# Routing the second FFN's first group of tokens inside the attention rounds

## What is computed

```python
logits = xf @ Wg
top_w, top_i = jax.lax.top_k(logits, TOP_K)
top_w = jax.nn.softmax(top_w, axis=-1)
...
h = jnp.einsum('nc,ech->enh', xf, W1)
g = jnp.einsum('nc,ech->enh', xf, W2)
y = jnp.einsum('enh,ehc->enc', jax.nn.silu(h) * g, W3)
out = jnp.einsum('enc,ne->nc', y, combine)
```

## Time and profile before

| | us |
|---|---|
| median of 3 runs | 816.96 |
| the runs | 812.55 to 818.23 |
| the profiled execution's own time | 811.2 |
| its span, first to last instruction | 809.4 |
| busy PE, DVE, ACT, POOL | 530.4, 531.9, 413.3, 204.9 |
| attention's DVE work ends at | 648.5 |
| the second FFN's block starts at | 670.4 |

### The profile page before, as it was taken

The page is one execution under the profiler, slowest core; times in us unless marked ns, Lnnn a source line. Parts: engine busy times, 40 slices in busy tenths (PEclk is TensorE's granted clock), DMA queues, the critical chain, the costliest instruction groups (busy, mean ns, idle before and its releaser), DMA issues. The chain is left out here.

```text
span 809.4 us, 14477 instructions
## 1 busy us (share of the span) xinstructions
PE 530.4 (66%) x5186; PEld 439.2 (54%) x5186; DVE 531.9 (66%) x1210; ACT 413.3 (51%) x909; POOL 204.9 (25%) x195
## 2 busy tenths in 40 slices
PE   5367567575666379999832578888868803878730
PEld 4256566464566278899832444454544503878720
DVE  2989989999996225575624477888875304654734
ACT  5576766778852254477633436767654202333320
POOL 1111221222215312607045240000000070163444
PEclk9567868867777769999975668999985655999985
DMA  8354456554562301223111400000000011134322
GB/s 242 79 150 122 145 156 172 156 151 124 155 170 83 99 7 57 72 70 106 43 43 26 157 0 1 2 2 1 2 1 1 1 49 43 49 97 114 86 69 58
DMA packets 98891, 63.96 MB, mean 79 GB/s; under 512 B 57218, under 2 KB 89476, under 8 KB 98692
## 3 DMA queue, kind: packets, MB, share of 16 engines
q1 hardware_dynamic: 94564, 54.12, 23.3%
q0 software_dynamic: 4256, 8.92, 3.8%
HBM read 40.33 MB, written 22.68 MB: 78 GB/s over the span
## 5 line engine op out<-in xcount | busy, mean ns | idle before, releaser
L1866 DVE TENSOR_REDUCE mx<-s_ps 128x2 f32<-128x512 f32 x128 | 82.4, 687 | 28.3 <-PE s_ps L1627 28.2
L1803 ACT ACTIVATE pt<-st_ps 128x512 f32<-128x512 f32 x128 | 69.7, 600 | 36.2 <-PE st_ps L1637 35.4
L336 POOL DMA_INDIRECT xd<-xs_all,r_posA x32 | 33.4, 1044 | 201.2 <-DVE r_posA L320 192.1
L1269 ACT ACTIVATE hid<-up,wblk 128x128 f32<-128x128 f32 x184 | 52.9, 375 | 49.6 <-PE up L1168 49.6
L630 ACT ACTIVATE tap<-cst_s,par 128x328 f32<-128x328 f32 x128 | 72.3, 654 | 3.8 <-DVE par L994 3.8
L637 ACT ACTIVATE rest<-rest,par 128x264 f32<-128x264 f32 x128 | 53.7, 504 | 29.9 <-DVE rest L941 29.9
L618 POOL TENSOR_TENSOR kst<-kst 128x504 f32<-128x504 f32 x16 | 16.4, 1026 | 181.3 <-DVE kst L869 181.3
L1627 PE MATMUL s_ps<-kf,qf 32*128 32x256 f32 x256 | 34.7, 349 | 31.0 <-DVE mx L1866 25.8
L336 POOL DMA_INDIRECT xd<-xs_all,r_posB x32 | 33.9, 1059 | 76.0 <-DVE r_posB L320 66.9
L1168 PE MATMUL up<-xsT,wblk 128*128 128x128 f32 x368 | 52.2, 288 | 0.0
L2145 DVE COPY wblk<-wslab 128x768 f32 x46 | 26.8, 585 | 38.1 <-issue 23.6
(11 more groups left out here) (364 smaller groups left out, 1375.5 us busy)
## 6 DMA issues: line engine op xcount, KB each, us to landing
kd<-kst SPq DMA_DIRECT2D x16, 512.0 KB, 3.0
xc<-in_x_coarse SPq DMA_DIRECT2D x16, 512.0 KB, 4.2
yd<-eos SPq DMA_DIRECT2D x44, 128.0 KB, 1.9
xsb<-xd SPq DMA_DIRECT2D x20, 256.0 KB, 3.4
wslab<-in_w SPq DMA_DIRECT2D x8, 578.0 KB, 4.7
dW<-kd SPq DMA_DIRECT2D x16, 256.0 KB, 3.3
wslab<-in_w SPq DMA_DIRECT2D x1, 3072.0 KB, 10.4
xd<-zero_t SPq DMA_DIRECT2D x2, 1472.0 KB, 11.1
```

The lines of the kernel that those rows point to most:

```text
L336: nc.gpsimd.indirect_dma_start(out=rows, out_offset=bass.IndirectOffsetOnAxis(ap=R.pos[:, t, k:k + 1], axis=0), in_=x[:, R.first + t, :], ...
L1269: nc.scalar.activation(hid[j % 2][:, k, :], up_ps[j % 2][:, k * P:(k + 1) * P], ACT.Gelu, bias=wblk[j % 4][:, 2 * DF + k:2 * DF + k + 1]). ...
L1803: nc.scalar.activation(pt[h % 8][:].rearrange("p t q -> p (t q)"), st_ps[k][:], ACT.Exp, scale=SCALE)\
L1866: nc.vector.tensor_reduce(mx[:, :, h:h + 1], s_ps[k][:].rearrange("p (t k) -> p t k", t=2), AX, ALU.max).then_inc(s_used, 1)
```

## The change

Group A of the second FFN is routed two rounds earlier. Its eight tiles are final when `projected(3)` has run at the head of round 6. In round 6 come the variances, the root (ACT, behind the fifth pair of exponentials), the rows, and the turning and columns of the first half; in round 7 the second half, the logits, largest, chosen, counted, prefix, ends and slots; in round 8 the owners. As `s_ps` is still in use then, all of it goes through the one bank `x_ps[2]`, half by half: a new function, `half_rows_turned`, turns four tiles into it. PE's `maxima`, which use that bank too, now wait in round 7 for the first columns and in round 8 for the positions. In the second FFN, B's turning moves from ahead of A's first rows to behind `up(1)`; DVE takes B's variances ahead of the first three `expert` copies and the columns behind `gated(0)`; logits and largest come at block 1, counted at 2, prefix and ends at 3, slots at 4, owners at 5.

```diff
--- before.py
+++ after.py
@@ -235,6 +235,14 @@
 
     v.wait_ge(R.turned, k + 1)
     nc.vector.tensor_copy(R.cols[:, k * CH:(k + 1) * CH], banks[k][:]).then_inc(R.cols_set, 1)
+
+
+def half_rows_turned(nc, pe, R, x, bank, k, ident):
+
+    pe.wait_ge(R.rows_set, 1)
+    for t in range(4 * k, 4 * k + 4):
+        last = nc.tensor.transpose(bank[:, t % 4 * P:(t % 4 + 1) * P], x[:, R.first + t, :], ident[:])
+    last.then_inc(R.turned, 1)
 
 
 def route_logits(nc, pe, R, bank, gate):
@@ -1697,6 +1705,10 @@
                     else:
                         pe.wait_ge(row_used, 1)
                     project(4 * i + 6)
+                if i == B - 1:
+                    pe.wait_ge(routes[0].cols_set, 1)
+                if i == B:
+                    pe.wait_ge(routes[0].pos_set, 1)
                 if i - 1 in whole:
                     pe.wait_ge(proj_used, min(4 * i + 6, PROJ))
                     maxima(i - 1, 1, 2)
@@ -1711,6 +1723,9 @@
                     project(4 * i + 7)
                 scores(i, 2)
                 values(i - 1, 0)
+                if i == B - 1:
+                    pe.wait_ge(max_added, 2 * i)
+                    half_rows_turned(nc, pe, routes[0], xs_all, x_ps[2], 1, ident)
                 scores(i, 3)
                 if i - 2 in whole:
                     if 4 * i + 6 < PROJ:
@@ -1723,10 +1738,9 @@
                     else:
                         pe.wait_ge(pj_used, i - 2)
                     by_token(i - 2, 1, 1)
-                if i == B:
-                    second_turned(nc, pe, routes[0], xs_all, s_ps, ident)
-                if i == B + 1:
-                    route_prefix(nc, pe, routes[0], s_ps[1], tri)
+                if i == B - 1:
+                    pe.wait_ge(ffn1_in, 32)
+                    route_logits(nc, pe, routes[0], x_ps[2], wgs)
                 scores(i, 4)
                 if 4 * i + 8 < PROJ:
                     if i >= 1:
@@ -1749,9 +1763,10 @@
                         pe.wait_ge(proj_used, 4 * i + 8)
                     value_rows(i + 1, 1)
                 scores(i, 6)
-                if i == B:
-                    pe.wait_ge(ffn1_in, 32)
-                    route_logits(nc, pe, routes[0], s_ps[0], wgs)
+                if i == B - 2:
+                    half_rows_turned(nc, pe, routes[0], xs_all, x_ps[2], 0, ident)
+                if i == B - 1:
+                    route_prefix(nc, pe, routes[0], x_ps[2], tri)
                 if 4 * i + 9 < PROJ:
                     pe.wait_ge(proj_used, 4 * i + 9)
                     project(4 * i + 9)
@@ -1823,13 +1838,13 @@
                 powers(i - 1, 0)
                 high(4 * i + 6)
                 powers(i - 1, 1)
-                if i == B:
-                    second_root(nc, act, routes[0], 1)
                 outputs(i - 2, 1)
                 high(4 * i + 7)
                 powers(i - 1, 2)
                 powers(i - 1, 3)
                 powers(i - 1, 4)
+                if i == B - 2:
+                    second_root(nc, act, routes[0], 1)
                 high(4 * i + 8)
                 powers(i - 1, 5)
                 if i + 1 in whole:
@@ -1916,40 +1931,44 @@
                     split(3)
                 projected(i - 3)
                 if i == B:
-                    second_variances(nc, link, routes[0], xs_all)
-                if i == B + 1:
-                    route_largest(nc, v, link, routes[0], s_ps[0], None)
-                    route_chosen(nc, link, routes[0])
-                    route_counted(nc, v, link, routes[0], it8)
+                    route_owners(nc, link, routes[0], blk, WROW)
                 largest(i, 1)
                 if i == 0:
                     split(4)
                     split(5)
                 split(4 * i + 6)
                 add_maxima(i - 1, 1, 2)
-                if i == B:
-                    second_rows(nc, v, link, routes[0], xs_all)
-                    for k in range(2):
-                        second_columns(nc, v, routes[0], s_ps, k)
                 largest(i, 2)
                 split(4 * i + 7)
+                if i == B - 2:
+                    second_variances(nc, link, routes[0], xs_all)
                 largest(i, 3)
+                if i == B - 1:
+                    second_columns(nc, v, routes[0], (None, x_ps[2]), 1)
                 if i == 0:
                     v.wait_ge(va_set, 6)
                 negated(i, 0)
                 largest(i, 4)
                 averaged(i - 2)
-                if i == B + 1:
-                    route_ends(nc, v, link, routes[0], s_ps[1])
-                    route_slots(nc, link, routes[0], s_ps[1])
-                    route_owners(nc, link, routes[0], blk, WROW)
+                if i == B - 1:
+                    route_largest(nc, v, link, routes[0], x_ps[2], None)
                 largest(i, 5)
+                if i == B - 2:
+                    second_rows(nc, v, link, routes[0], xs_all)
+                if i == B - 1:
+                    route_chosen(nc, link, routes[0])
+                    route_counted(nc, v, link, routes[0], it8)
                 split(4 * i + 8)
                 largest(i, 6)
                 add_maxima(i, 0, 0)
                 largest(i, 7)
                 split(4 * i + 9)
                 negated(i, 1)
+                if i == B - 2:
+                    second_columns(nc, v, routes[0], (x_ps[2],), 0)
+                if i == B - 1:
+                    route_ends(nc, v, link, routes[0], x_ps[2])
+                    route_slots(nc, link, routes[0], x_ps[2])
             projected(B - 1)
             v.wait_ge(row_added, 1)
 
@@ -2063,18 +2082,19 @@
                                             start=(k == 0), stop=(k == 1))
                 last.then_inc(eo_ready, 1)
 
-            second_turned(nc, pe, second, xs_all, rt_ps, ident)
             rows_turned(0)
             for j in range(TOTAL + 1):
                 if j < TOTAL:
                     if plan.opens(j) and pair_of[j] + 1 < len(PAIRS):
                         rows_turned(pair_of[j] + 1)
                     up(j)
+                if j == 1:
+                    second_turned(nc, pe, second, xs_all, rt_ps, ident)
                 if j >= 1:
                     down(j - 1)
-                if j == 0:
+                if j == 1:
                     route_logits(nc, pe, second, rt_ps[0], wgs)
-                if j == 4:
+                if j == 3:
                     route_prefix(nc, pe, second, rt_ps[1], tri)
 
         @block.scalar
@@ -2159,32 +2179,32 @@
                                                    R.rs[:, 0, t:t + 1], ALU.subtract, ALU.mult)
                 last.then_inc(y_ready, 1)
 
+            second_variances(nc, link, second, xs_all)
             for j in range(3):
                 expert(j)
-            second_variances(nc, link, second, xs_all)
+            second_rows(nc, v, link, second, xs_all)
             route_shares(nc, v, first)
-            second_rows(nc, v, link, second, xs_all)
-            for k in range(HALVES):
-                second_columns(nc, v, second, rt_ps, k)
             for j in range(TOTAL + 2):
                 if j < TOTAL:
                     gated(j)
+                if j == 0:
+                    for k in range(HALVES):
+                        second_columns(nc, v, second, rt_ps, k)
                 if j + 3 < TOTAL:
                     expert(j + 3)
-                if j == 0:
+                if j == 1:
                     route_largest(nc, v, link, second, rt_ps[0], None)
-                if j == 1:
                     route_chosen(nc, link, second)
                 if j == 2:
                     route_counted(nc, v, link, second, it8)
+                if j == 3:
+                    route_ends(nc, v, link, second, rt_ps[1])
                 if j == 4:
+                    route_slots(nc, link, second, rt_ps[1])
+                if j == 5:
+                    route_owners(nc, link, second, blk, WROW)
+                if j == 6:
                     route_shares(nc, v, second)
-                if j == 5:
-                    route_ends(nc, v, link, second, rt_ps[1])
-                if j == 6:
-                    route_slots(nc, link, second, rt_ps[1])
-                if j == 7:
-                    route_owners(nc, link, second, blk, WROW)
                 for m in range(first.n // 2):
                     if j == NB + 7 + 3 * m:
                         link(route_pair(nc, v, link, first, xs_all, m))
```

## The result

The changed kernel has a median of 777.20 us over four runs (775.47 to 779.75), the kernel before 815.92 beside it; the ratio is 0.953, 95% interval 0.948 to 0.958. Two later comparisons of the same two kernels gave 0.959 (0.954 to 0.963) and 0.957 (0.950 to 0.963), so it is 33 to 39 us faster; 29.1 were forecast, at 787.9 us.

What follows compares the result with a forecast made beforehand. Waits on POOL's scatters were taken to bound the kernel: some 22 us after attention, 5.28 in the second FFN. Block start -19.4 and B's rows -9.7 sum to -29.1, giving 787.9 us, range 776 to 800.

Steps and rivals of the forecast that it cites:

- round 6: Attention: added variances +2.4, root and rows together +1.3, columns and transposes nothing; +3.7 us, bounds 2.5 and 7.7.
- round 7: Attention: columns and logits +2.4, largest +1.1, chosen and counted +0.6, prefix +1.7, ends and slots nothing; +5.8 us.
- rounds 8 and 9: Attention without A's routing: transposes -1.8, logits -2.1, root and table loads -1.8, round 9 -1.9; -7.6 us, bounds -12 and -4.
- end of attention to the next block: With the scatter hidden, the next block starts about 0.5 us behind attention's own end, where some 22 us were waited.
- that to B's rows: Second FFN, block start to B's rows in PE: 50.0 us instead of 59.7, so -9.7; bounds -4 and -12.
- B's rows to the end: Second FFN, from B's rows in PE to the end of the span: 79.4 us, taken as unchanged.
- The hidden scatter: POOL's scatter of A runs beside rounds 8 and 9, ends near 642.6; next block starts at about 651.0 instead of 670.36.
- The second FFN: B's first scatter 24.2 us into the block instead of 33.8, B's rows at 50.0; the 5.28 us stall mostly goes.
- The rule on GpSimd's transfers: Scatters beside VectorE copies: by the skill's factor 4.8 us each, both scatters some 60 us longer; trace intervals grew 7%.
- the slow rival: Scatters beside VectorE slow, at 2.41 + 0.30 us each: span end 820.5, median 828 us. Chance 0.02.
- Half clock through round 7: Rival: PE at half clock all through round 7 costs 7 to 8 us more: 795.5 us. Chance 0.22.
- The added routing fits into idle time: Rival: rounds 6 and 7 cost 5 us instead of 9.5, block starts at 646.5: 783 us. Chance 0.2.

Runs made afterwards that it cites:

- repeats: The changed kernel unaltered, measured twice more beside other kernels on one chip: 781.89 us, ratio 0.959, and 779.83 us, ratio 0.957.
- without the variances: Changed kernel with group A's variances taken earlier, six tiles' statistics in round 5, the rest behind projected(3): 772.92 us, ratio 0.952.
- three pieces of round 8: Three kernels, each the changed kernel with one piece put back in round 8, result unread: root 779.84 us, logits 779.93, transposes 780.35.
- the scatter uncovered: Changed kernel, but POOL waits for the last projection's sum before scattering A, routing staying in rounds 6 and 7: 799.54 us, ratio 0.983.
- both edits: Changed kernel with the variances taken early and round 7's logits issued behind the fifth scores: 776.61 us, ratio 0.955.

## Why the prediction was right

The terms, in us, as forecast and as three profiles of the changed kernel show them:

| step | forecast | first profile | repeats |
|---|---|---|---|
| round 6 | +3.7 | +3.5 | +3.5, +3.5 |
| round 7 | +5.8 | +4.9 | +6.9, +6.9 |
| rounds 8 and 9 | -7.6 | -10.4 | -8.8, -8.8 |
| end of attention to the next block | -21.3 | -21.6 | -21.6, -21.6 |
| that to B's rows | -9.7 | -10.3 | -10.2, -10.0 |
| B's rows to the end | 0 | -1.0 | -1.1, -0.9 |
| sum | -29.1 | -35.0 | -31.3, -30.9 |

- *What bounds the kernel* was right, and so was the mechanism: both waits on a scatter are gone, and each pays alone.
- *The hidden scatter*: POOL was to start at 621.7 + 0.85 and end with 5.6 us to spare. It ended 2.9 us ahead of where it would have decided (644.76 + 2.24 against 649.92), 4.6 in the repeats, as rounds 8 and 9, which cover it, were shorter than forecast.
- *Round 6*: the total held, its split didn't. The root and the rows were put at 1.3; without the variances round 6 has its old length, the seventh maxima coming 1.5 later at full clock (591.62 - 577.95 = 13.7 against 587.39 - 575.25 = 12.1) and the rest being repaid, as the clock doesn't fall where it fell before. The variances were put at 2.4 and cost 3.5 with the clock that went with them. That the sum came out at 3.5 against 3.7 is in part luck: one term too small and one too large.
- *Round 7*: within the terms at either clock. The columns and logits ahead of the fifth scores cost the hole of 2.51 that 2.4 were set for; taking them away gave 1.5. The prefix, put at +0.9 at full clock and +2.7 at half, left DVE waiting 0.90 us before the eighth maxima in the first profile and 3.02 in the repeat, 0.29 before.
- *Rounds 8 and 9* is the term that was mis-sized: round 8 by nothing at equal clocks (5.7 forecast, 5.9 found), round 9 by one (1.9 forecast; 6.2 us instead of 9.05), and in the first profile 1.7 more since PE had the upper clock for some 3.5 us of round 8. The three pieces of round 8 measured 1.7, 2.3 and 1.8 at the lower level against 1.8, 2.1 and 1.8.
- *The second FFN*: the first scatter of B was forecast 24.2 us into the block and came at 23.9; B's rows at 50.0 and came at 49.3. That what follows B's rows would stay as it was missed 1.0.
- *The rule on GpSimd's transfers*: A's scatters came every (643.80 - 624.74)/15 = 1.27 us beside rounds 8 and 9, as when alone, B's every (694.35 - 674.15)/15 = 1.35 beside the copies, so the slow rival never showed. A's case is a weak test of it, as DVE was busy for only 2.44 of those 20.02 us; of B's scatters the longer ones took 1.16 to 1.33 us instead of 0.96. The Trainium skill's "SBUF — State Buffer", section "SBUF: two separate sides", has such transfers starve beside copies of VectorE that take the port they share; these rows show intervals at most 7% longer.
- *Half clock through round 7* came in part: 0.68 to 0.77, worth 2 us between repeats rather than 8. That the 0.50 of round 8 agrees with the rule named beside this rival isn't shown by its rows: PE was busy 23.45 of 27.46 us there, and 14.65 of 19.41 in round 6 at 0.91, though a matmul at the lower level is also busy for longer.
- *The added routing fits into idle time* was forecast at 783, nearer to the measured 777.20 than the forecast itself. That is luck: rounds 6 and 7 cost 8.4 to 10.4 us and not 5.
- The measured median stands 10.7 under the forecast. Of this, 1.0 is the median of before, which a fourth run took from 816.96 to 815.92, and 1.8 to 5.9 are the terms above. The rest isn't traced; as the later comparisons give 33 to 34 us instead of 38.7, it is likely the spread between executions. The median lies near the lower end of the stated 776 to 800, those of the repeats (781.89 and 779.83) further in.

## What to carry to other kernels

A transfer that one engine issues piece by piece is a stage of its own, and it is hidden by making its indices early enough, even where that makes the steps that do it longer: 8.4 to 10.4 us were added in rounds 6 and 7 to take 21.6 off the end. Once it is hidden, ask what it still bounds: from the head of round 8, where the positions are there, it needs 0.89 + 20.02 + 2.24 = 23.2 us to the next block. So what brings the positions earlier, in rounds 6 and 7, still pays in full up to that block, while rounds 8 and 9 gain nothing by getting shorter than 22.9 (23.2 less the 0.29 behind DVE; they took 21.8 to 22.6 us in the four profiles that ended on the scatter again). Count stages from the last common instruction, and put terms of PE beside each other only at the same granted clock.

## What was not expected of the hardware

- The same kernel had two lengths of rounds 7 and 8, 22.2 with 19.9 and 24.2 with 21.6 us, at granted clocks of 0.77 with 0.59 and 0.68 with 0.50, with the same instructions: 3.6 us of 780 that go with the clock. In four profiles of other kernels with the same work in round 8, that round took 16.3 to 16.5 us at 0.76 to 0.81.
- Pausing PE for 2.79 us in round 6, in a stretch of scores that leave it partly idle anyway, was followed by the lower level, and the round lost 1.1 us beyond the 2.4 of the variances; without the pause it kept 1.00. What made the clock rise in round 8 in some runs isn't settled.
- A block whose last instruction is a POOL scatter closes 2.24 us behind it (645.97 + 20.01 to 668.22 with the scatter uncovered, 638.77 to 641.02 with both edits, 668.12 to 670.36 before); one that ends on DVE closes in 0.29.
